# A two-layer vision block on one core: who multiplies the taps that GpSimd sums in the 5x5 convolution

## The reference, cut to what matters

```python
x = x + conv_ref(_gn(x), ...)            # group norm, then:
qkv = einsum('bchw,oc->bohw', x, qkv_w)  # 768 channels
agg = depthwise 5x5 convolution of qkv, padding 2
agg = grouped 8x8 pointwise convolution of agg
t = concat(qkv, agg); q = relu, k = relu, v
vk = v k^T (with a row of ones);  out = vk q, divided by its last row
out = projection to 256 channels, batch norm, added to x
```

## Time and profile before

| what | us |
|---|---|
| median of 3 runs (860.31 to 867.2) | 860.94 |
| the profiled execution, its own time | 862.0 |
| its span, first to last instruction | 860.2 |
| mean granted TensorE clock | 0.94 of full |
| convolution stage, VectorE's first tap to its last | 623.4 to 822.6 |

### The profile page before, as it was taken

How to read it: one execution, slowest core, us unless ns; L and a number is a source line. 1 busy time by engine, 2 the same in 40 slices (tenths; PEclk the granted TensorE clock), 3 DMA queues, 4 the chain that set the end, 5 groups by cost and what they waited for, 6 DMA issues and landing times.

```text
span 860.2 us, 25961 instructions
## 1 busy us (share of the span) xinstructions
PE 720.5 (84%) x11728; PEld 461.2 (54%) x11728; DVE 627.7 (73%) x471; ACT 430.0 (50%) x765; POOL 511.4 (59%) x201
## 2 busy tenths in 40 slices
PE   3797659656999799999999999797769878888998
PEld 1343324225899689887898897343323334323543
DVE  5692990245899798899899999136999996498522
ACT  1345245444878677678777773012533344544022
POOL 2011430252899788889889998210887996799000
PEclk9899688956999999999999999899989998999999
DMA  5000210018103611232321000500685883678101
GB/s 173 0 1 3 73 50 0 27 50 199 34 20 92 134 53 28 78 101 61 117 66 41 16 17 16 160 0 1 148 183 121 180 187 79 144 168 192 53 1 49
DMA packets 35970, 67.10 MB, mean 78 GB/s; under 512 B 15204, under 2 KB 16228, under 8 KB 35860
## 3 DMA queue, kind: packets, MB, share of 16 engines
q1 hardware_dynamic: 34900, 65.09, 30.6%
q10 hardware_dynamic: 960, 0.35, 0.2%
HBM read 28.91 MB, written 6.42 MB: 41 GB/s over the span
## 4 chain that ended last, share of the span: by engine, by line
PE 55%; DVE 21%; POOL 11%; ACT 6%; issue 4%; DMA 2%; SPq 0%; DVEq 0%; POOLq 0%; ACTq 0%
PE PS L938 18%; DVE PS L1377 8%; PE PS L840 5%; PE PS L1107 4%; POOL X L429 4%; PE PS L958 4%; PE PS L1040 3%; POOL WIN L429 3%; PE PS L981 3%; POOL arena L429 2%; PE PS L868 2%; PE PS L805 2%; PE PS L849 2%; PE PS L1052 2%; PE PS L1063 2%
## 5 line engine op out<-in xcount | busy, mean ns | idle before, releaser
L429 POOL TENSOR_TENSOR X<-X,spare 128x2048 f32<-128x2048 f32 x32 | 146.8, 4589 | 33.7 <-ACT mid L654 23.4
L938 PE MATMUL PS<-mid,arena 128*32 128x128 f32 x4096 | 136.6, 275 | 9.1 <-issue 8.2
L938 PE MATMUL PS<-APROD,arena 128*32 128x128 f32 x2048 | 133.2, 279 | 3.7 <-issue 3.4
L938 PE MATMUL PS<-WPR,arena 128*32 128x128 f32 x2048 | 133.2, 279 | 3.1 <-issue 1.3
L938 PEld LDWEIGHTS PS<-mid,arena 128*32 128x32 f32 x4096 | 120.6, 111 | 23.3 <-issue 14.8
L938 PEld LDWEIGHTS PS<-WPR,arena 128*32 128x32 f32 x2048 | 115.3, 112 | 15.0 <-issue 6.8
L938 PEld LDWEIGHTS PS<-APROD,arena 128*32 128x32 f32 x2048 | 114.0, 113 | 6.2 <-issue 5.9
L643 ACT ACTIVATE arena<-arena,small 128x512 f32<-128x512 f32 (+1 forms) x150 | 99.6, 712 | 25.9 <-DVE X L1267 12.3
L1377 DVE SCALAR_TENSOR_TENSOR PS<-arena,DW,PS 128x1024 f32<-128x1024 f32 x76 | 97.9, 1289 | 2.4
L429 POOL TENSOR_TENSOR WIN<-WIN,spare 128x2048 f32<-128x2048 f32 x16 | 73.4, 4587 | 9.3 <-DVE WIN L1267 7.5
L429 POOL TENSOR_TENSOR arena<-arena,spare 128x2048 f32<-128x2048 f32 x16 | 73.4, 4589 | 8.4 <-ACT mid L654 4.4
(11 more groups left out here) (172 smaller groups left out, 1410.0 us busy)
## 6 DMA issues: line engine op xcount, KB each, us to landing
arena<-arena SPq DMA_DIRECT2D x192, 153.0 KB, 3.4
arena<-dt_rows SPq DMA_DIRECT2D x56, 256.0 KB, 4.2
X<-in_x SPq DMA_DIRECT2D x4, 1024.0 KB, 7.9
dt_rows<-arena SPq DMA_DIRECT2D x8, 512.0 KB, 2.6
spare<-c_rows SPq DMA_DIRECT2D x64, 64.0 KB, 2.2
mid<-dt_rows SPq DMA_DIRECT2D x8, 256.0 KB, 3.3
out<-X SPq DMA_DIRECT2D x4, 512.0 KB, 2.6
WIN<-in_win SPq DMA_DIRECT2D x1, 1024.0 KB, 10.3
```

Source lines behind the costliest of these rows:

```text
L429: pool.tensor_tensor(HB[s % 4], HB[s % 4], CROW[:, k % 2:k % 2 + 1, :].broadcast_to([P, QN, HALF]), ALU.mult).then_inc(S["g_rd"], 1)
L938: mm = pe.matmul(PS[32 * n:32 * n + 32, 4 + i, j * P:(j + 1) * P], DXT[:, DT_ * b + g, 4 * h + j, 32 * i:32 * i + 32], DIAGB[k % 2][n][:, ...
```

## The change

For tiles n >= 3 ScalarE makes all four products, taps 1 to 4. They alternate between two buffers: `APROD` and `PROD`, which GpSimd no longer writes from tile 3 on. A product waits until GpSimd has added the product before the last one (L761's wait, now two back), and the first one into `PROD` waits until GpSimd has finished tile 2. GpSimd keeps the multiply of tap 0, the tap weights and the four adds.

ScalarE's order in tile n changes: products 1 and 2 of tile n + 2, then the evacuation of both halves, then the attention parts of half 0, product 3, the attention parts of half 1, product 4. Before, it was product 2, evacuation of half 0, parts of half 0, product 4, evacuation of half 1, parts of half 1.

```diff
         def by_scalar(n):
-            return (2, 4) if n >= 3 else ()
+            return tuple(range(1, POOL_TAPS[n])) if n >= 3 else ()
...
+        PRODUCTS = [(n, i) for n in range(B * QT) for i in by_scalar(n)]
+        PRODUCT_IN = (APROD[:, :, :], PROD)
...
-                        pool.tensor_tensor(POOL_SUMS[n % 2], POOL_SUMS[n % 2], APROD[:, :, :], ALU.add).then_inc(S["pool_add"], 1)
+                        pool.tensor_tensor(POOL_SUMS[n % 2], POOL_SUMS[n % 2], PRODUCT_IN[(others - 1) % 2], ALU.add).then_inc(S["pool_add"], 1)
...
             def product(n, i):
                 t, k = ORDER[n % QT], OTHERS[i]
-                done = scalar_products(n) + by_scalar(n).index(i)
-                if done:
-                    m = n if i == by_scalar(n)[1] else n - 1
-                    last = by_scalar(n)[0] if m == n else by_scalar(m)[1]
+                done = PRODUCTS.index((n, i))
+                act.wait_ge(S["pad_rd"], n + 1)
+                if done == 1:
+                    act.wait_ge(S["pool_add"], pool_adds(3))
+                elif done >= 2:
+                    m, last = PRODUCTS[done - 2]
                     act.wait_ge(S["pool_add"], pool_adds(m) + last)
-                act.activation(APROD[:, :, :], tap(t, k), ACT.Copy, scale=DW[:, t, k:k + 1]).then_inc(S["act_prod"], 1)
+                act.activation(PRODUCT_IN[done % 2], tap(t, k), ACT.Copy, scale=DW[:, t, k:k + 1]).then_inc(S["act_prod"], 1)

             for n in range(B * QT):
                 b, j = divmod(n, QT)
+                ahead = by_scalar(n + 2) if n + 2 < B * QT else ()
+                for i in ahead[0:2]:
+                    product(n + 2, i)
                 for c in range(2):
-                    if n + 2 < B * QT:
-                        for i in by_scalar(n + 2)[c:c + 1]:
-                            act.wait_ge(S["pad_rd"], n + 3)
-                            product(n + 2, i)
                     act.wait_ge(S["cv_ps"], 2 * n + c + 1)
...
+                for c in range(2):
                     act_between(n, c)
+                    for i in ahead[2 + c:3 + c]:
+                        product(n + 2, i)
```

## The result

| | before | with the change |
|---|---|---|
| median of 20 runs each, us | 864.71 | 859.54 |
| the profiled execution's span, us | 860.2 | 860.7 |
| ratio to before, 95% interval | | 0.9938 (0.9915 to 0.9961) |

The change makes the kernel 0.6% faster, 5.2 us by the medians; the forecast was 4.7 us. It lies within the 1% of which the prediction spoke. One of the 20 runs with the change took 1485 us and is left out of the ratio, which counts fast runs only. The kernel before came out at 864.71 here and at 860.94 in the three runs shown earlier. As a time, 859.54 is 3.2 above the forecast of 856.3, so I hold the difference and the ratio against the forecast.

The account below looks back on a forecast made before the run. No engine is full; the chain runs through VectorE alone to 707.87, then between TensorE, ScalarE and VectorE. Waits 4.2 plus evacuation 0.5 give 4.7 us: profiled 862.0 to 857.3, or 856.3 against the 860.94 median; range 851.5 to 862.0.

Parts of the forecast that it names:

- The eight waits: VectorE's on-chain waits for GpSimd at taps, shifts and first state product, tiles 1 to 5: 8.9 to 4.75, gaining 4.2 us.
- The layout: GpSimd's and VectorE's queues laid out tile by tile from measured durations, estimating each wait after the change: 4.75 us in all.
- The page's rule: A two-SBUF-input VectorE instruction and a GpSimd instruction reading SBUF exclude each other; the second to issue waits in full.
- random phases: Rival: VectorE meets GpSimd at random moments, mean wait 0.92 us, eight make 7.4; time 858.9, chance 0.18.
- The evacuation: Half-1 evacuation no longer delays the copy before the next transposes, once on the chain at 727.88: gain 0.5 us.
- TensorE's clock: Rival: TensorE hardly stands before its state matmuls, so its clock is higher, 1.9 us more; 854.4; clock and more 0.12.
- From tile 7 on: Later attention tiles: VectorE waits 0.9 us for GpSimd's sum, but the divide waits for ScalarE's reciprocal; gain 0.
- the cover of the divide: Slack before VectorE's divide, from tile 7 on: 0.33 us before plus 1.1, about 1.4 us a tile.
- the slower rival: Rival: late ScalarE products delay GpSimd's sums in tiles 8 to 11, 2.3 us over cover, costing 9.2; 865.5, chance 0.12.
- The no-gain rival: Rival: the waits stay or two-buffer products come no earlier, so only the evacuation counts; 860.4, chance 0.08.

Follow-up runs that it names:

- e2: The changed kernel with its four products and two buffers, but the evacuation in two parts again as before; ratio 0.9925 to the kernel before.
- e8: The changed kernel run once more, unaltered, as the measure for other runs; ratio 0.9925 to the kernel before.
- e10: The changed kernel plus two unread TensorE matmuls in the pause before the second attention step of tiles 6 to 9; ratio 0.9930 to before.
- e3: The changed kernel, with GpSimd given a value-preserving multiply ahead of adds 1 and 3 of each tile from 3 on; ratio 1.0039 to before.
- e4: The changed kernel, with GpSimd's four adds from tile 3 on covering only one of 32 image rows; ratio 0.9829 to before.
- e7: The changed kernel, with GpSimd's tap weights made ahead of add 4 and not add 3, from tile 3 on; ratio 0.9973 to before.
- e1: The kernel before with only the evacuation of both halves joined, old products in one buffer; ratio 0.9995 to before.
- e11: The kernel before plus two unread TensorE matmuls in the pauses of tiles 6 to 9; ratio 0.9974 to the kernel before.
- e5: The changed kernel with VectorE's four batch-norm shifts moved into its idle time ahead of tile 7; ratio 0.9970 to the kernel before.
- e6: The kernel before with VectorE's four batch-norm shifts moved into its idle time ahead of tile 7; ratio 1.0019 to the kernel before.

## Why the prediction was right

**The eight waits** were the step that carried it, and it held: 4.75 forecast, 4.98 measured, and 4.97 to 5.00 in `e2`, `e8` and `e10`. Term by term (forecast, measured): tile 1's shift 0, 0.06; tile 2 0.7 and 1.4, 0.57 and 1.62; tile 3 0.4 and 1.65, 0.30 and 1.87; tile 4 0.4, 0.30; tile 5 0 and 0.2, 0 and 0.27. The gain from them is 3.9 for 4.2. `e3` gives the cause (GpSimd's two multiplies back, gain gone) and `e4` the size of what was left.

The layout stopped one wait too early. The second state product, 2.24 with the change, lies on the chain once TensorE no longer hides it; the prediction doesn't name it.

**The page's rule** (the Trainium skill, "SBUF — State Buffer", "Who interferes with whom"): the runs agree. At 688.82 the tap waited 0.30 us where the add still ran 0.52, before 1.53 where it still ran 1.73, so it waits to within 0.2 of the add's end; the next add was held 3.23 - 2.36 = 0.87. But the prediction gives the rule for instructions with two inputs in SBUF, and the shifts and the state product read one tensor there. They waited all the same, 5.2 of the 8.9 us before, and ran nearly free when the adds were gone (`e4`). For them the layout rests on the rows and not on the rule. The rule didn't lead to random phases: `e7` moved 0.83 us of GpSimd's work and the waits moved as laid out. That rival falls; its 858.9 against 860.94 is 0.9976 too, outside the measured interval.

**The evacuation** was a term of 0.5; `e2` gives 0.3. It was sized by the issue distance of one instruction. Why less came of it isn't shown, and 0.3 is near the scatter of one profile.

**TensorE's clock** was a rival of 1.9 more, and half of it happened. TensorE's state matmuls, before and with the change:

```profile
707.91 5.48 PE L1020 MATMUL PS<-mid 128*128 128x129 f32 x32 [4.36 <-DVE WIN L1336]
```

```profile
709.84 2.05 PE L1029 MATMUL PS<-mid 128*128 128x129 f32 x16 [1.72 <-DVE WIN L1345]
712.27 2.05 PE L1029 MATMUL PS<-mid 128*128 128x129 f32 x16 [0.38 <-DVE WIN L1345]
```

Before, TensorE had stood 4.36 us and made them at a granted clock of 0.69; with the change it had stood 1.72 and made them at 1.00. That is 5.48 - 4.10 = 1.4 us, and 0.4 is given back while the second group waits for the ninth wait. From the masked state's end to tile 5's L1112 it was 14.1 before (15.2 in `e1` and `e11`, at a clock of 0.5) and 13.1 in the four profiles of the change, `e2`, `e8` and `e10`. So 1.0 came on top against the profile shown: 3.9 + 1.0 + 0.4 by tile 6 (0.3 of it the evacuation, by `e2`) = 5.3, the whole of the difference. The forecast put this term at 0 and gave the evacuation 0.5 and the waits 4.2, so part of the agreement between 4.7 and 5.2 is luck.

**From tile 7 on** the gain was put at 0, and the distance stayed 14.08. The sum is what VectorE waits for, 1.17 for 0.9 forecast. But the cover of the divide was put at 1.4 and is 0.53 (0.33 before). The forecast let the tap run freely after its wait; it met GpSimd's next multiply and was held 0.8 more. Here the slower rival came nearest. Two other margins were thin too. The last add of tile 8 was over at 755.15, 0.1 before VectorE started that tile, so product 2 ended when the evacuation was due. And product 3, issued at 760.34, came 0.8 after GpSimd's first add (over at 759.54), for the 1.5 laid out. Nothing was paid, but the room that I saw wasn't there.

**The no-gain rival** falls with `e1` and `e2`: the waits fell, and by the products.

## What to carry to other kernels

When two engines share a port, list each meeting of their instructions on the critical chain and ask where the other engine stands at that moment; its busy share doesn't tell. Laying out the queues from measured durations gave each of eight waits to about 0.2 us here, and missed by 0.6 to 1.8 us when whole instructions were moved (`e5`, `e6`). Carry the list past the point where the chain changes engines: a wait that was hidden can come out. Freeing an engine pays only through such meetings and through waits that end last. Where both engines were busy for most of a tile, taking 7.3 us off one of them brought the first masked state 2.1 us forward (4.6 of 7.1 in the old kernel), and nothing that the run times show.

## What the runs showed of the hardware

The port waits repeat from one execution to the next far better than the whole time does. Their sum was 4.97 to 5.00 us in four profiles of three kernels, while the 20 runs of the change scattered from 850 to 863 us (one outlier at 1485). How tile 2's share splits between tap and shift does change: 0 and 2.19 in the profile of before, 1.47 and 0.74 in `e11`, whose work up to there is the same.

TensorE's granted clock over the state matmuls went with how long it had stood before them: 1.72 us and 1.00 in four profiles; 4.36 and 0.69 before; 4.4 and 0.5 in `e1` and `e11`; 4.15 and 0.61 in `e5`. But `e7` had stood 2.50 and had 1.00, `e3` 2.59 and had 0.7, so these pairs don't settle what decides it; no run changed that pause alone.

A good part of the scatter of the run times can come from tiles whose TensorE ran partly at 1.2 GHz: each costs 1.6 us, and a profile had none to three of them among tiles 6 to 10. What decides it stays open. A single profile's stage length must be read tile by tile before an edit is blamed for it; `e1` and `e7` would else have been taken for losses of 4 to 5.5 us.
